# Edge chunks of the scatter pass: 628 in place of 640, as 39 loop bodies of 16 and a rest of 4 written out

## The reference, cut to what matters

```python
def _propagate(all_emb, rows, cols, vals):        # 18750 nodes, 250000 edges
    acc = all_emb
    x = all_emb
    for _ in range(3):
        x = jax.ops.segment_sum(vals[:, None] * x[cols], rows, num_segments=N_NODES)
        acc = acc + x
    return acc / 4
...
light_out = _propagate(all_emb, graph_rows, graph_cols, graph_vals)   # 64 features
mm_out = _propagate(mm_all, graph_rows, graph_cols, graph_vals)       # 16 features, repeated to 64
rating = users_emb @ items_emb.T + bias_user[users] + bias_item.T     # 1024 x 12500
return jax.nn.sigmoid(rating)
```

## Time and profile before

| | us |
|---|---|
| timed runs | 6974.55, 6979.57, 6995.24; median 6979.57 |
| the profiled execution, its own time | 6999.02 |
| its span, first to last instruction | 6996.9 |
| mean granted clock of TensorE | 0.773 of full |
| scatter passes of layers 0, 1, 2 (stretches of the trace) | 1342, 1193, 1232 |
| VectorE busy in them | 762, 685, 684 |
| folds of layers 0, 1, 2 | 532, 530, 527 |

### The profile page before, as it was taken

One profiled execution on the slowest core, in us unless ns is written; L12 is line 12 of the kernel. 1 busy time (PEld: TensorE's weight loads), 2 busy tenths in 40 slices (PEclk: granted clock), 3 DMA queues, 4 the chain that ended last, 5 costly groups with the idle time before them and its releaser, 6 DMA issues.

```text
span 6996.9 us, 176879 instructions
## 1 busy us (share of the span) xinstructions
PE 4049.9 (58%) x58024; PEld 3417.5 (49%) x58262; DVE 5232.6 (75%) x7719; ACT 4117.8 (59%) x10170; POOL 2357.1 (34%) x2110
## 2 busy tenths in 40 slices
PE   5301111156677666776666666677666666667776
PEld 4300111056566555665555556566555555556652
DVE  9999999965555555999555555699955555559997
ACT  0155555244444445998555555699855555559986
POOL 0144332044444444000555555400055555550000
PEclk9755555577777777999777787799977777779998
DMA  9400000044444445664444444466444444446669
GB/s 340 193 0 0 0 0 0 6 128 141 142 142 144 141 144 141 161 162 125 139 144 139 144 145 143 145 162 162 124 139 139 140 135 139 138 136 157 162 168 313
DMA packets 740582, 931.05 MB, mean 133 GB/s; under 512 B 68989, under 2 KB 585886, under 8 KB 740144
## 3 DMA queue, kind: packets, MB, share of 16 engines
q1 hardware_dynamic: 647552, 675.42, 34.4%
q0 software_dynamic: 92672, 254.01, 10.1%
q10 hardware_dynamic: 304, 1.00, 0.1%
HBM read 539.05 MB, written 391.19 MB: 133 GB/s over the span
## 4 chain that ended last, share of the span: by engine, by line
DVE 37%; issue 26%; PE 15%; another core or an unknown queue 13%; ACT 4%; DMA 2%; DVEq 2%; POOL 0%; SPq 0%; POOLq 0%; ACTq 0%
DVE ring L1220 9%; PE psum L1455 7%; DVE store L1012 5%; DVE ring L1176 4%; PE psum L1457 4%; DVE ring L1259 3%; PE psum L1492 2%; DVE store L990 2%; DVE total L807 2%; ACT ring L659 2%; DVE store L991 2%; DVE ring L1253 2%; DVE new L1268 2%; DMA out<-new 1%
## 5 line engine op out<-in xcount | busy, mean ns | idle before, releaser
L649 ACT ACTIVATE ring<-ring 128x64 f32<-128x64 f32 x7680 | 1920.3, 335 | 1840.7 <-DVE ring L1176 1148.9
L725 POOL DMA_INDIRECT posts<-ring x1920 | 1939.1, 1010 | 3139.5 <-ACT ring L649 2665.3
L1455 PE MATMUL psum<-store,ring 128*128 x15360 | 2239.7, 262 | 1030.7 <-DVE ring L1220 608.9
L1455 PEld LDWEIGHTS psum<-store,ring 128*128 128x128 bf16 x15360 | 1841.8, 124 | 1195.0 <-issue 1166.7
L1176 DVE TENSOR_REDUCE ring<-psum 128x512 f32<-128x1024 f32 x960 | 1173.3, 1222 | 1572.8 <-remote 1515.2
L1457 PE MATMUL psum<-store,ring 128*128 x15360 | 2153.8, 229 | 166.1 <-issue 163.7
L1457 PEld LDWEIGHTS psum<-store,ring 128*128 128x128 bf16 x15360 | 1662.0, 115 | 246.8 <-issue 204.9
L1220 DVE TENSOR_SCALAR ring<-ring,lane_f 128x1024 bf16<-128x1024 bf16 x1920 | 860.7, 490 | 10.2 <-DMA ring<-lanes_d 10.2
L1486 PE MATMUL psum<-ring 128*128 128x64 bf16 x7584 | 560.4, 198 | 230.4 <-DVE ring L1253 226.5
L708 POOL TENSOR_TENSOR ring<-store 128x1024 f32<-128x1024 f32 x157 | 370.3, 2359 | 799.2 <-DVE store L991 363.7
L1492 PE MATMUL psum<-ring 128*128 128x64 bf16 x15168 | 529.4, 194 | 153.1 <-DVE ring L1259 150.9
(11 more groups left out here) (232 smaller groups left out, 3973.6 us busy)
## 6 DMA issues: line engine op xcount, KB each, us to landing
ring<-lanes_d SPq DMA_DIRECT2D x480, 512.0 KB
ring<-posts SPq DMA_DIRECT2D x240, 516.0 KB
store<-posts SPq DMA_DIRECT2D x234, 516.0 KB
out<-new SPq DMA_DIRECT2D x96, 500.0 KB, 8.3
posts<-store SPq DMA_DIRECT2D x2, 20640.0 KB, 115.8
posts<-store SPq DMA_DIRECT2D x2, 20124.0 KB, 88.6
posts<-ring POOLq DMA_INDIRECT x1920
ring<-runs_d SPq DMA_DIRECT2D x80, 256.0 KB
```

The lines of the kernel that those rows point to most:

```text
L649: last = nc.scalar.activation(of, of, ACT.Copy, scale=vring[:, h, c * BLOCK + b:c * BLOCK + b + 1])
L725: pool.indirect_dma_start(out=posts[:, :], out_offset=bass.IndirectOffsetOnAxis(ap=dring[:, h, c:c + 1], axis=0), in_=msg[:, n, :], in_off ...
L1455: pe.matmul(psum[:, c, b * 2 * F:(b + 1) * 2 * F], of, xflat[:, bass.ds(at_d[c] * F + k * XT, 2 * F)], start=(k == 0), stop=False, skip_gr ...
```

## The change

CH0 becomes a multiple of 4: 140 in place of 128. The pass visits 628 chunks, one of them empty. They are done as 39 bodies in the loops and a rest of 4 chunks (two pairs, half h = 0), which every engine has written out behind its loop, once in each layer. The bodies of the loops stay as they are; their helpers take the number of chunks as a parameter. In layer 0 the last full body now compares the runs and looks up for the rest (4 chunks in place of 8). The counts that the semaphores are compared with follow: a layer has 79 halves (HALVES), 79 loads of the first lane buffer and 78 of the second (HALF_LOADS), and sends 316 and 312 chunks by the two halves of the ring, times 16 (SENT_ROWS: 5056 and 4992). The two joins that are left after the loop write to slots 0 and 1 of the ring in place of 6 and 7. The fold is not touched.

```diff
-CH0 = SKIP // 16 * 16
+CH0 = SKIP // 4 * 4
 CHUNKS = CHUNKS_M - CH0
 BODIES = CHUNKS // 16
+REST = CHUNKS - BODIES * 16
+HALVES = 2 * BODIES + 1
+HALF_LOADS = [HALVES, HALVES - 1]
+SENT_ROWS = [16 * (8 * BODIES + REST), 16 * 8 * BODIES]
...
+                def lanes(i, h, n):
+                    if layer == 0:
+                        sp.wait_ge(s_rhot, i * 2 + (h + 1))
+                        sp.sem_inc(s_sppace, 1)
+                        sp.dma_start(runs_r[:, 0:n * P], ...).then_inc(s_drow, 16)
+                    for b in range(n // 4):
+                        sp.wait_ge(s_hots, i * 8 + (layer * DUOS + h * 4 + b * 2 + 2))
+                        sp.sem_inc(s_sppace, 1)
+                        sp.dma_start(idx[b], ...).then_inc(s_idx[b], 16)
                 with sp.Fori(0, BODIES) as i:
                     for h in range(2):
...
+                        lanes(i, h, 8)
+                lanes(BODIES, 0, REST)
                 for h in range(2):
-                    sp.wait_ge(s_scat[h], 128 * BODIES * (layer + 1))
+                    sp.wait_ge(s_scat[h], SENT_ROWS[h] * (layer + 1))
...
+                with act.Fori(0, BODIES) as i:
+                    scale_chunks(i, 16)
+                scale_chunks(BODIES, REST)
...
+                with pool.Fori(0, BODIES) as i:
+                    scatter(i, 16)
+                scatter(BODIES, REST)
...
-                def refill(i, h, first):
+                def refill(i, h, first, n):
...
-                        dve.wait_ge(s_scat[h], i * 128 + layer * BODIES * 128)
+                        dve.wait_ge(s_scat[h], i * 128 + layer * SENT_ROWS[h])
...
-                    nc.vector.tensor_copy(dring[:, h, :], dest_m[:, at])
+                    nc.vector.tensor_copy(dring[:, h, 0:n], dest_m[:, at])
...
+                def send(i, first, final=False, pairs=8):
+                    for d in range(pairs):
+                        h, j = d // 4, d % 4
...
+                        if j == 1:
+                            n = min(8, 2 * pairs - 8 * h)
+                            if layer == 0:
+                                place(i, h, n)
+                            refill(i, h, first, n)
+                        if first and d < SPLITS:
+                            take(layer, d)
+                        if layer == 0 and j == 2:
+                            run_hots(i * 32 + 16 * (h + 2), i * 2 + (h + 1), REST if final and h == 1 else 8)
...
                     send(BODIES - 1, False, True)
+                    send(BODIES, False, pairs=REST // 2)
                 else:
                     send(0, True)
                     with dve.Fori(1, BODIES) as i:
                         send(i, False)
+                    send(BODIES, False, pairs=REST // 2)
                 for d in range(2):
-                    join((layer + 1) * DUOS + d + 1, 6 + d)
+                    join((layer + 1) * DUOS + d + 1, d)
...
-                        if layer == 0 and n % 8 == 7 and not (final and n == 15):
-                            look_up(i + n // 8, 1 - n // 8)
+                        if layer == 0 and n % 8 == 7:
+                            look_up(i + n // 8, 1 - n // 8, REST if final and n == 15 else 8)
...
                     sums(BODIES - 1, True)
+                sums(BODIES, chunks=REST)
```

More of the change, by code:

```diff
@@ L56 @@
 B_LEN = (HALF - B_FIRST) * WIDE
-assert CH0 % 4 == 0 and BODIES * 16 == CHUNKS and 0 < B_EDGE < WIDE
+assert CH0 % 4 == 0 and REST == 4 and 0 < B_EDGE < WIDE
 PIECE_P = [(P0, HALF, HALF + P0), (HALF, 2 * HALF, 0), (2 * HALF, ROWS_M, 2 * HALF)]
@@ L639, in _, with scale_chunks @@
                     cast_two(layer, q)
-                with act.Fori(0, BODIES) as i:
-                    for n in range(16):
+                def scale_chunks(i, chunks):
+                    for n in range(chunks):
                         h, c = n // 8, n % 8
                         if c == 0:
-                            act.wait_ge(s_ringed, i * 2 + (layer * BODIES * 2 + h + 1))
+                            act.wait_ge(s_ringed, i * 2 + (layer * HALVES + h + 1))
                         if n % 2 == 0:
@@ L719, in _, with scatter @@
                 done = layer * CHUNKS
-                with pool.Fori(0, BODIES) as i:
-                    for n in range(16):
+                def scatter(i, chunks):
+                    for n in range(chunks):
                         h, c = n // 8, n % 8
@@ L1176, in join, with run_hots @@
                     nc.vector.tensor_reduce(msg_sums[:, d, :, :].rearrange("p a (e f) -> p a e f", f=F), sums, AX.X, ALU.add).then_inc(s_added, 1)
-                def run_hots(landed, looked):
+                def run_hots(landed, looked, n=8):
                     dve.wait_ge(s_drow, landed)
@@ L1183, in run_hots, with place @@
                     for k in range(2):
-                        last = nc.vector.tensor_scalar(rhot[:, k, :], runs_r, lane_f[:, k:k + 1], None, ALU.is_equal)
+                        last = nc.vector.tensor_scalar(rhot[:, k, 0:n * P], runs_r[:, 0:n * P], lane_f[:, k:k + 1], None, ALU.is_equal)
                     last.then_inc(s_rhot, 1)
-                def place(i, h):
+                def place(i, h, n):
                     dve.wait_ge(s_looked, i * 2 + (h + 1))
-                    nc.vector.tensor_reduce(found[:, h, :], psum[:, 4 + h, 0:8 * PARTS].rearrange("p (c x) -> p c x", x=PARTS),
+                    nc.vector.tensor_reduce(found[:, h, 0:n], psum[:, 4 + h, 0:n * PARTS].rearrange("p (c x) -> p c x", x=PARTS),
                                             AX.X, ALU.add).then_inc(s_found, 1)
                     dve.wait_ge(s_found, i * 2 + (h + 3))
-                    nc.vector.tensor_tensor(dest_m[:, bass.ds(i * 16 + h * 8, 8)], found[:, h, :], dest_m[:, bass.ds(i * 16 + h * 8, 8)],
-                                            ALU.add).then_inc(s_placing, 1)
-                def refill(i, h, first):
+                    at = bass.ds(i * 16 + h * 8, n)
+                    nc.vector.tensor_tensor(dest_m[:, at], found[:, h, 0:n], dest_m[:, at], ALU.add).then_inc(s_placing, 1)
+                def refill(i, h, first, n):
                     dve.wait_ge(s_msg, i * 16 + (done + h * 8 + 8))
@@ L1208, in refill @@
[L1208 to L1230, removed]
@@ new lines, in refill @@
+                    at = bass.ds(i * 16 + h * 8, n)
+                    nc.vector.tensor_copy(dring[:, h, 0:n], dest_m[:, at])
+                    nc.vector.tensor_copy(msg_lanes[:, h * 8:h * 8 + n, :, :], lanes_m[:, at, :].rearrange("p s (a e) -> p s a e", e=2))
+                    nc.vector.tensor_copy(vring[:, h, 0:n * BLOCK].rearrange("p (s e) -> p s e", e=BLOCK), vals_m[:, at, :]).then_inc(s_ringed, 1)
+                def send(i, first, final=False, pairs=8):
+                    for d in range(pairs):
+                        h, j = d // 4, d % 4
+                        dve.wait_ge(s_sent, i * 8 + (layer * DUOS + d + 1))
+                        if not (first and d < 2):
+                            join(i * 8 + (layer * DUOS + d + 1), (d + 6) % 8)
+                        if j % 2 == 0:
+                            dve.wait_ge(s_idx[j // 2], i * 32 + (layer * HALF_LOADS[j // 2] + h + 1) * 16)
+                        for k in range(2):
+                            last = nc.vector.tensor_scalar(hot[d % 2][:, k, :], idx[j // 2][:, j % 2 * 2 * CHUNK:(j % 2 + 1) * 2 * CHUNK],
+                                                           lane_f[:, k:k + 1], None, ALU.is_equal)
+                        last.then_inc(s_hots, 1)
+                        if j == 1:
[7 more added lines that the diff above has]
+                            run_hots(i * 32 + 16 * (h + 2), i * 2 + (h + 1), REST if final and h == 1 else 8)
@@ L1429, in supers, with look_up @@
                         max_val=(SUPERS - 1) * 2 * PARTS, skip_runtime_bounds_check_because="the chip clamps each above")[1]
-                def look_up(i, h):
+                def look_up(i, h, chunks=8):
                     pe.wait_ge(s_rhot, i * 2 + (h + 2))
                     pe.wait_ge(s_found, i * 2 + (h + 1))
-                    for m in range(8):
+                    for m in range(chunks):
                         if m % 4 == 0:
@@ L1441, in look_up, with sums @@
                     last.then_inc(s_looked, 1)
-                def sums(i, final):
-                    for n in range(16):
+                def sums(i, final=False, chunks=16):
+                    for n in range(chunks):
                         d, c = n // 2, n % 4
@@ L1460, in sums @@
                             last.then_inc(s_sent, 1)
-                        if layer == 0 and n % 8 == 7 and not (final and n == 15):
-                            look_up(i + n // 8, 1 - n // 8)
+                        if layer == 0 and n % 8 == 7:
+                            look_up(i + n // 8, 1 - n // 8, REST if final and n == 15 else 8)
                 if layer:
                     with pe.Fori(0, BODIES) as i:
```

(2 more changed lines are left out.)

12 lines of the change are left out of this document (2 added, 10 removed).

## The result

| | before | after |
|---|---|---|
| timed runs, median | 6992.23 us (6974.55 to 7027.63, 5 runs) | 6890.78 us (6878.81 to 6908.07, 5 runs) |
| the profiled execution's span | 6996.9 us | 6906.3 us |
| mean granted clock | 0.773 | 0.774 |

The ratio is 0.9856, with an interval of 0.9825 to 0.9887: 101 us less, between 79 and 122. The forecast was 67 us less. The direction and the range (6889 to 6937) held, but the size was too small: 67 us is a ratio of 0.9904, outside the interval.

A forecast was written before the change was run, and what follows sets the result against it. The prediction took a TensorE-VectorE chain to bound the passes. Removed chunks, 68.0 us, less seams, 1.1 us, gave 66.9 us saved, set against the median 6979.57 us: 6912.7 us, range 6889 to 6937 for 8 in 10.

The forecast's parts named there:

- The bound: In the three passes over edge chunks: a TensorE-VectorE chain over two buffers binds, no engine near full; removed chunks save their time.
- The pace as price: In the passes: a removed half of 8 chunks saves the mean pace, 16.62, 14.79 and 15.25 us in passes 1 to 3.
- The removed 1.5 halves: 12 of 640 chunks out of each pass: 70.0 us saved by mean pace, 65.9 us counted from the pass ends.
- a sign of being wrong: In the passes: the prediction is wrong if they shorten by less than 15 us each.
- the 68.0 us: Saving of the removed chunks over all three passes, taken as the middle of 70.0 and 65.9 us.
- Rival 2: Loops moved in memory keep another pace: 6948.7 us if pass 2 slows (0.13), 6876.7 if pass 3 quickens (0.09); together 0.22.
- The seams: From loop to written-out code on five engines, once a pass: 0.36 us added each, 1.1 us in all.
- Rival 1: Slow seams: fetching fresh code behind the loop holds up every pass by 4.3 us, 6924.4 us in all; chance 0.08.
- Rivals 3, 4 and 5: In the passes: cheap removed chunks, 6918.6 us (0.03); disturbed halves for good, 7081 us (0.03); no effect, 6980 us (0.02).
- Kept once a pass: Behind the last join of each pass: last scalings, scatters and landing stay the same whatever the number of chunks; no term.

The follow-up runs named there:

- c4: Kernel before with 624 chunks a pass in loops of 39 bodies, no rest, on the quick chip: 6013.10 us, ratio 0.9879 against before.
- d4: Kernel before with 16 more empty chunks a pass, 656 in 41 bodies: 7088.55 us, ratio 1.0121 against before.
- e1: Kernel before with all 640 chunks, as 39 bodies and a written-out rest of 16, on a slow-pace chip: 6906.51 us, ratio 0.9985 against before.
- e2: Kernel before with 624 chunks a pass in loops, no rest, on a slow-pace chip: 6801.11 us, ratio 0.9834 against before.
- d1: Kernel before, unchanged, run again on a slow-pace chip: 6988.67 us, ratio 0.9997 against before.
- d2: Changed kernel run again on a slow-pace chip: 6906.54 us, ratio 0.9866 against before.
- d3: Kernel before with 86 empty TensorE matmuls written out behind the passes of layers 0 and 1: 7004.77 us, ratio 1.0005 against before.
- c3: Kernel before with all 640 chunks, as 39 bodies and a written-out rest of 16, on the quick chip: 6088.36 us, ratio 0.9998 against before.
- f2: Kernel before with all 640 chunks, as 39 bodies and a written-out rest of 16, on another slow-pace chip: 7007.79 us, ratio 0.9981 against before.
- f1: Kernel before, unchanged, run again on another slow-pace chip: 7021.29 us, ratio 0.9996 against before.

## Why the prediction was right or wrong

- **The bound** was right. A chain between TensorE and VectorE carries the passes, and no engine hid the removed chunks: on every chip removing chunks paid at least their share.
- **The pace as price** held in part. Two halves a pass less brought 73.6 us for 70.2 worked out (c4), two more cost 85 us for 92.9 (d4, its interval 64 to 105), and e1 to e2 differed by 93.3 us in the profiles for 91. It was too low for the changed kernel each time, 101 us for 70, 94 for 70 and 67 for 53, each outside the interval, and for e2 against before, 115 us for 91 to 93, just outside.
- **The removed 1.5 halves, 70.0 by the mean pace, 65.9 by the ends**: in pass 1 the pass got 24.3 us shorter for 24.9 or 25.3. In pass 2 it was 15.5 us (12.4 us from d1 to d2, under the 15 us that I had named as a sign of being wrong) for 22.2 or 20.1, in pass 3 55.4 us (58.4 us from d1 to d2) for 22.9 or 20.5. The step that failed is the one behind the 68.0 us: that the paces of before stay. In its place the runs showed another pace in pass 3, 14.81 and 14.78 us a half in place of 15.25 and 15.17. Together the passes gave 95.2 us.
- **Rival 2**, the other pace, was the case that came about, in the direction that I had given 0.09: pass 3 took on pass 2's pace, 36 us by my sum, and 6876.7 us in all. The time was 6890.8. Its cause as I gave it, the new place of the loops in memory, found no support: TensorE's code shifted kept the time (d3), the rest of 16, which shifts all engines' code, moved it by 0.2% at most (c3, e1, f2), and unchanged code changed its pace (pass 2 of d1 against that of f1). I had hung this rival on the Trainium skill's rule on fetch after taken branches (Runtime: NRT & Kernel Launch, section on instruction fetch). Whether instruction supply is what TensorE lacks in those gaps no run here shows, so the rule is neither borne out nor refuted as this chip's pace setter.
- **The seams**, 1.1 us: too small to be measured here, and nothing larger shows. The joins behind the rest began after 3.52 us of idle time in pass 1, while TensorE still worked, and after 0.48 to 1.18 us before the last ones of passes 2 and 3. Rival 1 (4.3 us a pass, a ratio of 1.002) is out by c3, 0.9998 with 0.9989 to 1.0007, and at the slow pace by e1 and f2, whose intervals end at 1.0005 and 1.0002.
- **Rivals 3, 4 and 5**: cheap empty chunks would have saved 61 us, below the interval of 79 to 122; slower and no change didn't come.
- **Kept once a pass**: right at the slow pace; on the quick chip the wait for the last scatters is up to twice as long and was 4.4 us shorter in pass 3 after the change.

What stays open: why both pairs of profiles at the slow pace have the slow pass 3 only before the change. Chance in single executions, theory A, doesn't carry it: the medians hold it too, 94 and 101 us over eleven runs of the changed kernel, where chunks alone give 70. Nor does the clock of whole executions: the profiled pairs had 0.773 and 0.774, and 0.777 and 0.775. If the form brings the 10 to 13 us that e1 and f2 point to, some 82 us are explained, which lies inside both intervals; but neither of these two is clear of zero, and e2 won about 22 us beyond its chunks without the form. Several profiled executions of each kernel on one chip would tell chance from cause; that wasn't tried.

## What to carry to other kernels

Where two engines hand work to and fro and neither is near full, price a removed loop step at the measured pace of the whole loop. The busiest engine's time would have understated it by a third (TensorE's 759 us in 80 halves are 9.5 us, of 14.8). The pace was right within some 10 us a pass in passes 1 and 2, and missed by 32 to 36 us in pass 3. Take that pace from several profiles: one profile's difference between two passes of the same code (14.79 and 15.25 us here) may be a spread, as pass 2's 14.69 to 14.96 us in unchanged code shows, and belongs into the range. State the range as a saving too, since the time before moves between measurements (6979.57 and 6992.23 us here). And padding to the granularity of the loop body can be dear: 12 empty chunks of 640 cost 1.1 to 1.4% here, and a short rest written out behind the loop had no price that could be measured.

## What the runs showed of the hardware

The same program took 6087 us on one chip and 6919, 7001 and 7023 us on three others, by the medians of the kernel before; in the first measurement it was 6992 us. The stages outside the passes agree: the stretch from the last join of pass 1 to the first ring copy of pass 2 was 562.8 us on the first chip (3318.05 less 2755.29) and 564.1 us on the quick one. The passes alone differ, and in them TensorE's idle time put down to issue and its clock. The timeline of such a place on the first chip, in the long half of the earlier trace rows: one matmul every 0.72 us (from 5408.19 on, two), with nothing waited for, where 41 of them fit in 3.00 us in the earlier trace rows, 0.07 us each.

```profile
5406.75 0.20 PE L1457 MATMUL psum<-store,ring 128*128 x1 [0.51 <-issue]
5407.47 0.29 PE L1455 MATMUL psum<-store,ring 128*128 x1 [0.51 <-issue]
5408.19 0.21 PE L1457 MATMUL psum<-store,ring 128*128 x1 [0.43 <-issue]
```

The idle time put down to issue, 185 us in pass 2 on the first chip (137.4 + 47.2) and 4 us on the quick one, covers some 180 of the 301 us by which the 79 halves differ, (14.79 - 10.98) x 79. What starves TensorE there the runs don't tell. Most of the rest is TensorE's work itself, busy for 759 us in pass 2 at a mean granted clock of 0.76 on the first chip and for 615 us at 0.88 on the quick one:

```profile
3045.00:3932.00 887.00, 614.55 (x10242) 0.88 0.69 189
```

Within one chip the time of an execution goes with its clock as well. Of the 35 executions of the kernel before on the chip of d1, the ten with a mean clock of 0.767 or less had a median of 7019 us, the twelve with 0.772 or more one of 6985 us. That is as much as the extra of the change. But all six of d2, at 0.768 to 0.775, took 6892 to 6924 us, and so lie below all of the 35 (6974 to 7040).

Whether the jump back of TensorE's loop costs anything stays open. The halves that cross it took 14.40 us in the mean of pass 2 in the first profile, the others 15.18 us; on the quick chip it was 11.43 against 10.54 us, the other way round.
